# A decoder layer on one core: the first feed-forward weight of the second half turned another way

## What is computed

```python
x = layernorm(x + self_attention(x))            # over 8 positions, 512 columns, 16 heads of 32
x = layernorm(x + cross_attention(ctx_2048, x, mask))   # 8 batches of 512 x 512, 8 heads of 64
h   = relu(einsum('bsd,hd->bsh', x, w1) + b1)   # w1: 2048 x 512, float32
hq  = float_quantize(h, 4, 3)
wq  = float_quantize(w2, 4, 3)                  # w2: 512 x 2048
out = einsum('bsh,dh->bsd', hq, wq) + float_quantize(b2, 5, 10)
x = layernorm(x + float_quantize(out, 5, 10))
```

## Time and profile before

| | |
|---|---|
| median of 3 runs | 1871.29 us (1870.2 to 1871.86) |
| profiled execution, its own time | 1870.93 us |
| its span, first to last instruction | 1869.1 us |
| mean granted clock of TensorE | 0.987 of full speed |
| busy share of the span | PE 95%, PEld 52%, DVE 74%, ACT 41%, POOL 30% |

### The profile page before, as it was taken

How to read it: one execution, slowest core, us unless ns; L and a number is a source line. 1 busy time by engine, 2 the same in 40 slices (tenths; PEclk the granted TensorE clock), 3 DMA queues, 4 the chain that set the end, 5 groups by cost and what they waited for, 6 DMA issues and landing times. The chain is left out here.

```text
span 1869.1 us, 32453 instructions
## 1 busy us (share of the span) xinstructions
PE 1775.7 (95%) x12432; PEld 978.3 (52%) x12432; DVE 1374.0 (74%) x1466; ACT 770.5 (41%) x1208; POOL 566.8 (30%) x578
## 2 busy tenths in 40 slices
PE   7999999999999998978899999999999999999988
PEld 3665456545654564634545555455454554554543
DVE  2899999999999999957566577575675666657721
ACT  3323222222232222237657265373562744726522
POOL 3125865596559525600100302003011020030000
PEclk9999999999999999999999999999999999999999
DMA  9436346535653467556430613405205143051010
GB/s 217 128 74 136 97 124 153 130 79 137 148 123 85 118 143 184 156 147 201 103 74 2 142 46 74 113 1 130 57 14 134 40 106 81 1 137 28 13 34 23
DMA packets 295166, 183.86 MB, mean 98 GB/s; under 512 B 194015, under 2 KB 251359, under 8 KB 295038
## 3 DMA queue, kind: packets, MB, share of 16 engines
q1 hardware_dynamic: 287392, 178.50, 38.3%
q10 hardware_dynamic: 7646, 3.50, 1.0%
HBM read 94.82 MB, written 33.62 MB: 69 GB/s over the span
## 5 line engine op out<-in xcount | busy, mean ns | idle before, releaser
L1223 POOL TENSOR_TENSOR q<-q,x_hi 128x512 f16<-128x512 f32 x28 | 40.5, 1475 | 597.5 <-ACT x_hi L1571 597.5
L1251 PE MATMUL b_ff<-x2T_hi,w1T_hi 128*128 128x512 f16 x512 | 195.3, 381 | 2.3 <-DVE x2T_lo L1661 2.3
L1251 PE MATMUL b_ff<-x2T_lo,w1T_hi 128*128 128x512 f16 x512 | 195.3, 381 | 0.0
L1251 PE MATMUL b_ff<-x2T_hi,w1T_lo 128*128 128x512 f16 x512 | 195.1, 381 | 0.0
L1661 DVE TENSOR_TENSOR p_lo<-k,p_hi 128x1024 f16<-128x1024 f32 x128 | 161.3, 1260 | 37.4 <-ACT p_hi L1517 37.4
L1550 ACT ACTIVATE k<-b_st,mbias 128x512 f32<-128x512 f32 x256 | 161.9, 693 | 41.4 <-PE b_st L1318 37.9
L1711 DVE SCALAR_TENSOR_TENSOR top<-b_st,mleast,top 128x512 f16<-128x512 f32 x168 | 126.1, 751 | 51.5 <-PE b_st L1278 34.5
L825 DVE TENSOR_TENSOR prod<-q,k 128x4096 f32<-128x4096 f32 x32 | 143.0, 4469 | 20.7 <-ACT q L691 19.9
L607 PE MATMUL sm_b<-cT_hi,wsT_hi 128*128 128x256 f16 x512 | 141.1, 276 | 14.7 <-DMA cT_lo<-rows_lo 12.2
L457 POOL TENSOR_TENSOR rows_lo<-cn,rows_hi 128x512 f16<-128x512 f32 x64 | 131.4, 2061 | 61.0 <-ACT rows_hi L675 61.0
L571 PE MATMUL pj_b<-winT_hi,xT_hi 128*128 128x512 f16 x384 | 148.1, 386 | 0.9 <-DVE winT_lo L892 0.9
(11 more groups left out here) (287 smaller groups left out, 4314.1 us busy)
## 6 DMA issues: line engine op xcount, KB each, us to landing
cn<-in_ctx_dram SPq DMA_DIRECT2D x64, 256.0 KB, 3.3
k<-kT_scratch SPq DMA_DIRECT2D x24, 512.0 KB, 7.9
x<-in_x_dram SPq DMA_DIRECT2D x32, 256.0 KB, 3.1
x_scratch<-x SPq DMA_DIRECT2D x32, 256.0 KB, 2.3
q<-x_scratch SPq DMA_DIRECT2D x8, 1024.0 KB, 5.6
q<-x_scratch SPq DMA_DIRECT2D x32, 256.0 KB, 2.8
out_dram<-q SPq DMA_DIRECT2D x32, 256.0 KB, 3.3
xn<-in_x_dram SPq DMA_DIRECT2D x24, 256.0 KB, 2.9
```

What stands on the lines that cost most here:

```text
L1251: mm = pe.matmul(out, a, c, start=(start and n == 0), stop=end)
```

## The change

w1 no longer goes through TensorE, ScalarE and VectorE. GpSimd scales each raw tile by 64 in place (float32), copies it to float16 (the high rows, in `x1_hi`), and writes the difference as low rows over the raw tile. SP then turns both with two transposing transfers into `w1T` (`turn_w1`). w2 still goes the old way, and TensorE's wait is now only for its own bank. `load_weights` becomes `load_w1` and `load_w2`, and SP's order is new. ScalarE waits for all turns of w1 before it writes batch 1's high rows, and TensorE before the first feed-forward product. Later waits on `x1_turned` have a constant added.

```diff
+    w1_row_lo = [z[:, 2 * i, :] for z in x2T for i in range(2)]
...
+    W1_TURNS = 32 * FT // 4
...
+            def load_w1(n):
                 if n >= 4:
-                    sp.wait_ge(s["w1_filled"], n - 3)
+                    sp.wait_ge(x1_turned[n % 4], 32 * (n // 4))
                 sp.dma_start(w1_n[n % 4], d.w1[n * P:(n + 1) * P, :]).then_inc(w1_ld[n % 4], 16)
+
+            def turn_w1(n):
+                sp.wait_ge(s["w1_row_lo"], n + 1)
+                for dst, rows in ((w1T[0], x1_hi[n % 4][:, :]), (w1T[1], w1_row_lo[n % 4])):
+                    sp.dma_start_transpose(col(dst, n), rows).then_inc(x1_turned[n % 4], 16)
+
+            def load_w2(n):
                 if n >= 4:
                     sp.wait_ge(s["w2_filled"], n - 3)
...
-            for n in range(2):
-                load_weights(n)
-            for g in range(len(GROUPS)):
-                queries(0, g)
-            for n in range(2, 4):
-                load_weights(n)
+            for n in range(4):
+                load_w1(n)
+            load_w2(0)
+            load_w2(1)
+            turn_w1(0)
+            turn_w1(1)
+            queries(0, 0)
+            queries(0, 1)
+            turn_w1(2)
+            queries(0, 2)
+            load_w2(2)
+            load_w2(3)
             load_x1(1, True)
+            for n in range(4, FT):
+                load_w1(n)
+                turn_w1(n - 1)
+                load_w2(n)
+            turn_w1(FT - 1)
             for tt in range(4):
                 load_residual(0, tt, True)
-            for n in range(4, FT):
-                load_weights(n)
...
+            for n in range(FT):
+                pool.wait_ge(w1_ld[n % 4], 16 * (n // 4 + 1))
+                if n >= 4:
+                    pool.wait_ge(x1_turned[n % 4], 32 * (n // 4))
+                pool.tensor_scalar(w1_n[n % 4], w1_n[n % 4], WS, None, ALU.mult).then_inc(s["w1_scaled"], 1)
+                pool.wait_ge(s["w1_scaled"], n + 1)
+                pool.tensor_copy(x1_hi[n % 4][:, :], w1_n[n % 4]).then_inc(s["w1_row_hi"], 1)
+                pool.wait_ge(s["w1_row_hi"], n + 1)
+                pool.tensor_tensor(w1_row_lo[n % 4], w1_n[n % 4], x1_hi[n % 4][:, :], ALU.subtract).then_inc(
+                    s["w1_row_lo"], 1)
...
             def weight_transposes(n):
...
+                pe.wait_ge(w2_ld[n % 4], 16 * (n // 4 + 1))
+                if n >= 2:
+                    pe.wait_ge(s["w2_done"], n - 1)
+                transposes(ff_b[n % 2], w2_n[n % 4], s["w2_filled"])
...
+                if f == 0 and i == 0 and isinstance(b, int) and b == 0:
+                    for t in x1_turned:
+                        pe.wait_ge(t, W1_TURNS)
...
-                hi(col(w1T[0], n), bank4(ff_b[n % 2]), s["w1_filled"], n + 1, s["w1_hi"], WS)
...
+                for t in x1_turned:
+                    act.wait_ge(t, W1_TURNS)
                 x1_rows_high(1, True)
...
             def first_heads():
-                w1_low(0)
...
-                    w1_low(2 * h + 1)
                     exponentials_low(0, h, 1)
-                    if h + 1 < H2:
-                        w1_low(2 * h + 2)
```

More of the change, by code:

```diff
@@ L1076, in phase_b @@
              "l3_stats", "l3_mv", "l3_rstd", "l3_done", "m_ld", "k_ld", "v_ld",
-             "rows_ld", "cols_ld", "made", "rows_made", "step", "w1_filled", "w1_hi", "w1_lo",
+             "rows_ld", "cols_ld", "made", "rows_made", "step", "w1_scaled", "w1_row_hi", "w1_row_lo",
              "w2_filled", "w2_done")
@@ L1132, in load_x1 @@
                     for tt in range(4):
-                        sp.wait_ge(x1_turned[tt], 32 * (b - 1))
+                        sp.wait_ge(x1_turned[tt], W1_TURNS + 32 * (b - 1))
                 stand_alone(sp, alone["sp"])
@@ L1158, in store @@
                 sp.dma_start(out_o[b, tt], x2[:, tt, :]).then_inc(out_st[tt], 16)
-            def load_weights(n):
+            def load_w1(n):
                 if n >= 4:
-                    sp.wait_ge(s["w1_filled"], n - 3)
+                    sp.wait_ge(x1_turned[n % 4], 32 * (n // 4))
                 sp.dma_start(w1_n[n % 4], d.w1[n * P:(n + 1) * P, :]).then_inc(w1_ld[n % 4], 16)
+            def turn_w1(n):
[3 more added lines that the diff above has]
+            def load_w2(n):
                 if n >= 4:
@@ L1267, in queries @@
                     for tt in range(4):
-                        pe.wait_ge(x1_turned[tt], 32 * b)
+                        pe.wait_ge(x1_turned[tt], W1_TURNS + 32 * b)
                         stand_alone(pe, alone["pe"])
@@ L1370, in output_x1 @@
                         else:
-                            pe.wait_ge(s["w2_done" if tt == 2 else "w1_lo"], FT)
+                            pe.wait_ge(s["w2_done"], FT - 3 + tt)
                     products(om_b[tt][:, :], [t for j in range(KT) for t in terms([col(z, tt)[:, j] for z in x1T],
@@ L1532, in weights_high @@
             def weights_high(n):
-                hi(col(w1T[0], n), bank4(ff_b[n % 2]), s["w1_filled"], n + 1, s["w1_hi"], WS)
                 act.wait_ge(s["w2_filled"], n + 1)
-                act.activation(w2_dst(n), bank4(ff_b[1 - n % 2]), ACT.Copy, saturate=False).then_inc(s["w2_done"], 1)
+                act.activation(w2_dst(n), bank4(ff_b[n % 2]), ACT.Copy, saturate=False).then_inc(s["w2_done"], 1)
             def relu(b, f):
@@ L1568, in x1_rows_high @@
                     if not first:
-                        act.wait_ge(x1_turned[tt], 32 * (b - 1))
+                        act.wait_ge(x1_turned[tt], W1_TURNS + 32 * (b - 1))
                         stand_alone(act, alone["act"])
@@ L1661, in low @@
                 dve.tensor_tensor(dst, bank, hi, ALU.subtract).then_inc(out, 1)
[L1663 to L1669, removed]
             def moments(l, x, n, i):
```

## The result

The changed kernel takes 1893.8 us in the median of 4 runs (1891.77 to 1897.51), beside 1871.57 for the kernel before. The ratio is 1.0116, 95% interval 1.0097 to 1.0135: 22 us slower. The forecast was 1885.5, range 1876 to 1895, so the direction held and the size was 8 us short. The time lies 1.2 us inside the upper end of the range, and also in the range of the rival "GpSimd is slow", so the number alone doesn't tell these two apart.

The account below looks back on a forecast made before the run. Bound: a loop through several engines, 8.15 us a head, no engine full. 1870.93 us plus 13.6 for w2's last tile (start included, heads' gain lost) plus 1.0 for the clock gave 1885.5; range 1876 to 1895.

Parts of the forecast that it names:

- GpSimd is slow: Rival, chance 0.14: one-input instructions cost what the subtraction does and p_lo blocks them; step over 11.5 us, time 1891 to 1898.
- The start: Before batch 0's first scores: turns of w1's tiles 0 and 1 hold SP, so the queries' copies start 8.4 us later.
- One w1 tile on GpSimd: Cast and multiplication 0.62 us each, subtraction 1.155: 2.7 us a tile, 3.1 in the heads; ends 2.0 and 4.9.
- The tile chain: In SP's loop, turn, w2's load, w1's landing and GpSimd follow in a row: 9.8 us per two tiles, 13.6 us later.
- GpSimd and VectorE: In the heads, p_lo meeting a GpSimd instruction loses 0.4 us, leaving 0.27 of the 0.67 us gain a head.
- the gain is lost in the wait: In batch 0's heads, the gain of 2.5 to 5.3 us disappears in TensorE's wait for late w2 tiles.
- ScalarE's new wait for the turns: After the heads: the last turn lands at about 928, ScalarE's wait comes at about 930 and costs nothing.
- The clock: TensorE's output product behind the last head may start at half clock: zero to 2 us, taken as 1.
- Only the start counts: Rival, chance 0.17: the tile chain keeps up, with a step under 8 us; time 1874.0 to 1876.8.

Follow-up runs that it names:

- loads ahead: The changed kernel with w1's load n + 1, in place of load n, issued ahead of turn n - 1 in SP's loop: 1885.73 us, ratio 1.0061.
- four loads first: The kernel w2 first, with w1's tiles 2 and 3 loaded after query groups 0 and 1, not before: 1872.10 us, ratio 1.0001.
- w2 first: Changed kernel, SP's batch 0 order rewritten: queries 0, 1 and w2's tiles 2, 3 before turns, w1 loads one tile further ahead, rows after turn 9: 1871.79 us.

## Why the prediction was right, and where it was short

- **The start** was right in kind and 2.7 us short: 11.1 us at the first scores against 8.4. w1's tile 0 reached GpSimd 18.9 us into the half, against 18.1, and two tiles cost GpSimd 3.9 and 3.4 us, not 2.7 each.
- **One w1 tile on GpSimd** is the term that was mis-sized. The cast was priced right and the multiplication at 0.62 in place of 1.49 us, from a memset and a cast, though the bound above was 1.155. So even the upper end for a single one-input instruction was too low. A tile in the heads took 3.8 us against 3.1. Left out, the multiplication gave 6.3 us back.
- **The tile chain** was right, step by step: turn, w2's load, w1's load, landing 3.1 to 3.9 (3.5 forecast), GpSimd. The step was 10.6 in place of 9.8 us, and the 0.7 us by which the GpSimd tile was priced too low is nearly all of that. With loads ahead it fell to 7.96. Tile 4 was done at 56.0 us into the half in place of 49.9: 3.1 because its load was issued later (2.7 of it from the start), 2.7 because the load landed in 7.8 us and not in 5.2, the rest the tile's own price. Five steps and tile 4 together make 9.7 of the shortfall, and a w2 load that landed sooner gave a little back: TensorE turned the last tile 22.7 us later in place of 13.6.
- **GpSimd and VectorE.** The forecast was right: a gain of 0.67 us a head, of which 0.27 remains where the `p_lo` on the loop meets GpSimd. With SP's order mended a head gained 0.71 us without a collision and 0.22 with a full one, and such a `p_lo` lost 0.48 us, against 0.4. In the changed kernel itself this played no part, since the waits for w2 hid the loop, and its `p_lo` was hardly held up. GpSimd lost as well, 0.4 us a tile there (3.80 in the mean against 3.40 alone), as taken. Beside 48 subtractions back to back, on the kernel before, VectorE lost only in the first and the last head; what decides which side loses was not taken apart.
- **That the gain is lost in the wait** was right. ScalarE's new wait for the turns cost nothing; it split batch 1's rows directly behind the last `p_hi`. The clock cost nothing behind the last tile, where 1 us was taken: from TensorE's turn of that tile to the output split it is 14.8 us (940.33 to 955.10) and was 14.7 (912.51 to 927.23), both at a granted 1.00.
- **The rivals.** Slow GpSimd, at 0.14, gave 1891 to 1898 and a step over 11.5 us. The time fell in its range as well as in mine, and its price for the multiplication was the nearer one. The step of 10.6 and the cast at half the subtraction's cost are not that case. That my range held is in part luck: with the multiplication at more than twice its price, it held by 1.2 us. "Only the start counts" was given easier terms than the forecast's own sum has: from 9.8 us, a step under 8 needs a tile of 1.3 us or a landing of 1.7, not 2 or 2.5. Here the step was what counted.

## What to carry to other kernels

Work moved to an idle engine isn't free if its results pass through a queue with other customers: here each turn stood ahead of a load that TensorE needed, and a load stood behind the turn that it should have overtaken. Draw the queue's order as a recurrence, with one landing time for each load that isn't issued ahead. When the moved work comes off a loop through several engines, expect a good part of it to turn into waits. And when one of several equal instructions stands on the loop, read that one: the median over all `p_lo` stayed at 1.22 us while the one that set the pace took 1.70.

## What the runs showed that I had not expected

- GpSimd's `tensor_scalar` on 128x512 float32 took 1487 ns at least. The cast from float32 to float16 of that size took 609, and the two-input subtraction 1152.
- Who loses between GpSimd and VectorE differs by the place. Beside 48 subtractions back to back `p_lo` was as without them in the even heads, and GpSimd did the waiting. With w1's three instructions in one stream the second `p_lo` of a head took 1.70 us in place of 1.23 in most heads, and the head grew by as much.
- Small instructions of VectorE can be held up too: beside the subtractions one `mz` took 0.98 us in place of 0.18.
- A gain at the start can be lost to the clock: with four loads first, the source bias ran at a granted 0.62, where w2 first, whose scores start 2 us later, had 1.00. What brought the lower clock isn't shown; the kernel before started earlier still and made these products as fast as w2 first.
